# A pre-norm transformer block on one core: normalisation on another engine, masks of the last query block on VectorE, a reordered start and end

## The chip, the cores and the metric

One core of a Trainium2 chip runs the whole program. The time is the device time of one execution in microseconds (us). A core has five engines that run in parallel and meet at semaphores: TensorE (PE, matmuls), VectorE (DVE), ScalarE (ACT), GpSimd (POOL) and SyncE (SP, which here only starts DMAs). TensorE writes to eight PSUM banks of 128 partitions by 512 f32.

## The reference

Eight sequences of 512 tokens with 128 channels go through attention (16 heads of 8 channels, causal) and a feed-forward part with 8 experts that all tokens pass, each weighted by a gate.

```python
def reference(x, w_qkv, b_qkv, w_proj, b_proj, Wg, bg, W1, b1, W2, b2):   # x: 8 x 512 x 128
    x = x + attn(layernorm(x))
    x = x + ffn(layernorm(x))
# attn: q, k, v = split(x @ w_qkv + b_qkv), 16 heads of 8
#       softmax(where(causal, q k^T / sqrt(8), -inf)) v, then @ w_proj + b_proj
# ffn:  probs = sigmoid(x @ Wg + bg);  weights = probs * (probs > 0.5)      # 8 experts
#       h = relu(x @ W1[e] + b1[e])        # 512 hidden
#       sum over e of weights[:, e] * (h @ W2[e] + b2[e])
```

## The kernel before

**Split matmuls.** Where f32 precision is wanted at the speed of the shorter format fp32r, an operand is split in a high part (ACT writes it) and a low part (DVE or POOL subtracts), and three matmuls are added up (L1107 to L1109).

**Attention.** Heads are taken in 4 groups of 4 a sequence. `stack` holds q and k of a group in 32-row pieces, so that the scores of several heads run in different rows of the array at once; even groups lie in rows 0 to 63, odd ones in rows 64 to 127. A group has 10 "max" units and 10 "exp" units, each one PSUM bank. A max unit computes scores with queries on the partitions, adds the causal mask by one more matmul with an identity (L1178, array form 128x128, where the scores' form is 32x128), and DVE takes the negative row maximum (L1018). Units 0 to 3 of a group hold the last query block (`qb == 3`) of one head: 512 keys, of which the last 128 get a mask. Units 4 to 9 hold query blocks 2, 0 and 1. The maxima go through POOL (`nm`, L740, L742), a matmul (L1238), ACT (L819) and two DMAs (L655) into a row of `stack`, so that the exp unit, which computes the scores again with keys on the partitions, has them subtracted. ACT takes the exponential (L831), POOL zeroes the blocks over the diagonal (L755), and 16 small matmuls multiply with v (`pv`, L1248, form 128x32). Then transposes (L1113), a division (L1034, L1038), the projection (L1264).

**A visit** is one call of `scores` on PE: two max units and two exp units that lie some units behind (`EXP_LAG`, 12; 18 for the first 50 units), both or one of them (L1146 to L1179). With 10 units a group, 12 units behind is the group before for 4 of 5 visits, and for the fifth the group before that, which lies in the same rows of the array.

**Layer norm.** DVE computes the statistics (L901, L905), POOL the reciprocal root in two operations (`rs1`, `rs2`: L713, L716), DVE applies both (`ln1n`, `ln2n`: L910, four operations of 128x128), and PE transposes the result (`xT`, `x2T`).

**Feed-forward part.** 32 slots a sequence (8 experts by 4 pieces of the hidden layer). A slot is `z` (three matmuls), ACT's relu into `h_hi` (L863), the low part by DVE (L1070) or, for 12 of 32 slots, by ACT and POOL (L869, L762), and `y` (three matmuls into `y_bank`, L1293 to L1297), which waits for the low part before its first matmul. After four slots DVE multiplies by the gate (`term`, L1083) and POOL adds up (`acc`, L772). `h_hi` and `h_lo` have three buffers.

**What sets the order.** Nothing is scheduled on the chip: `list_schedule` (L279) plays the program through with booked costs and due times when the program is built, and writes down each engine's fixed order. `FFN_LAG` sets how many slots the feed-forward part of a sequence lies behind its attention. Where PE has nothing to do before the first feed-forward work, the list gets `warm` matmuls (L1193), whose result nobody reads. Until then, max units, exp units and W1 preparation share eight banks, afterwards seven and `y_bank`.

**Start.** W1 and the gate weights are multiplied by a centring matrix (`w1`, `small`: L1204 to L1212, ACT L789, DVE L953), to take the mean out of the layer norm. Before the first scores stand the memsets of `stack` on DVE (L878, L879), the load of x, layer norm, transposes, q and k, and the DMAs of `stack` (L641, L644).

Of the kernel before, what the change touches and what calls it, by code (L numbers as in the profile page):

```python
# [44 lines left out]
N_U = len(MAX_UNITS)  # L45
CHUNK_END = (3, 7, 9)
# [5 lines left out]
PT_SLOTS = 14  # L52

# [7 lines left out]
EXP_LAG = 12  # L61
HEAD_LAG, HEAD_UNITS = 18, 50
FFN_LAG = 54
# [4 lines left out]
ENTER = {"full": 190, "mask": 92, "scores": 190, "pv": 98}  # L68
SWITCH_DUE = 1.5
PV_DUE = 2  # L70
# [6 lines left out]
SHIFT = {('act', 'exp', False): 2,  # L77
         ('act', 'hhi', False): 3.5,
         ('act', 'nm', True): -5.5,
         ('dve', 'hlo', False): -7.0,  # L80
         ('dve', 'ln1a', False): 10.0,
         ('dve', 'ln2n', False): 8.5,
         ('dve', 'merge', True): 8,
         ('dve', 'smax', True): -7.5,
         ('dve', 'v', True): 7.5,
         ('dve', 'w1', False): 3.5,
         ('pe', 'ex', True): -9,
         ('pe', 'gate', False): -2.0,
         ('pe', 'gate', True): 0.5,
         ('pe', 'k', False): -4.5,  # L90
         ('pe', 'k', True): -4,
         ('pe', 'nm', False): -35.5,
         ('pe', 'oT', False): -1.5,
         ('pe', 'xT', False): 3,
         ('pe', 'y', False): 1,
         ('pe', 'y', True): 0.5,
         ('pool', 'causal', True): -11.0,
         ('pool', 'nm', True): -14.5,
         ('sp', 'mrow', False): -11}


def visits():

    units = [(i, g, u) for i in range(BATCH) for g in range(GROUPS) for u in range(N_U)]
    result, done = [], 0
    for k in range(0, len(units) + EXP_LAG, 2):
        lag = HEAD_LAG if k <= HEAD_UNITS else EXP_LAG
        while done < k - lag:
            result.append(([], [("ex", *n) for n in units[done:done + 2]]))
            done += 2  # L110
        ex = units[done:done + 2] if done <= k - lag else []
        done += len(ex)
        result.append(([("max", *n) for n in units[k:k + 2]], [("ex", *n) for n in ex]))
    return result


def work_items():
# [20 lines left out]
    put("pool", ("mask", None), -60, 1300)  # L138
    put("pool", ("center", None), -13, 4500, ("pool", ("rs1", 0)))
    put("dve", ("wqk", None), -19.9, 1500, ("dma", ("wqkv", None)), ("dve", ("ln1b", 0)))  # L140
    put("dve", ("b1", None), -13.9, 4200, ("dma", ("small", None)), ("dve", ("klo", 0)))
    put("dve", ("vset", None), -10, 1800, ("dve", ("klo", 0)))
    put("pe", ("small", None), 20, 1500, ("pool", ("center", None)))
    put("dve", ("small", None), 20, 700, ("pe", ("small", None)))
    for e in range(EXPERTS):
        put("pe", ("w1", e), 10 + 2 * e, 1300, ("dma", ("w1", None)), ("pool", ("center", None)),
            ("dve", ("b1", None)), ("pe", ("k", 0)))
        put("act", ("w1", e), 10 + 2 * e, 600, ("pe", ("w1", e)))
        put("dve", ("w1", e), 10 + 2 * e, 690, ("act", ("w1", e)))
# [1174 lines left out]
```

## Time and profile before

| | us |
|---|---|
| median of 3 runs | 685.77 (685.29 to 686.74) |
| the profiled execution | 686.17 |
| its span, from the first to the last instruction | 684.4 |
| PE busy | 650.2 (95%) |
| DVE busy | 480.8 (70%) |
| ACT busy | 418.6 (61%) |
| POOL busy | 330.9 (48%) |

The profiled execution has 1.8 us outside its span, and is 0.4 us above the median. A PE instruction's busy time overlaps the next one's, so what a matmul costs on PE's path is the distance from its start to the start of the next instruction. In a row "x4" stands for four like instructions in a row.

### The profile page before, as it was taken

What the parts mean: (1) busy time and instruction counts of PE and PEld (TensorE: products, weight loads), DVE (VectorE), ACT (ScalarE), POOL (GpSimd) and SP (SyncE); (2) the same over time, 40 slices, a digit from 0 to 9 for tenths busy, and PEclk for the clock granted to TensorE, in tenths of its full rate; (3) what the DMA queues carried; (4) which work ended last, traced back from release to release, by engine and by line L of the source; (5) the groups of instructions that cost most, each with busy time, mean ns of one, the idle gap of its engine ahead of it and who ended that gap; (6) DMA issues with size and microseconds to landing.
All of it is one profiled execution on the core that took longest, in us unless ns stands there. A gap on an engine that the chain in (4) does not pass through costs nothing.

```text
span 684.4 us, 13158 instructions
## 1 busy us (share of the span) xinstructions
PE 650.2 (95%) x4486; PEld 449.4 (66%) x4486; DVE 480.8 (70%) x958; ACT 418.6 (61%) x793; POOL 330.9 (48%) x409
## 2 busy tenths in 40 slices
PE   2799999999999989999999989999999999999996
PEld 2355666667666766667666756667666766677774
DVE  5797687679876796669866696668866676546443
ACT  2158656667666666676666566666666666665553
POOL 4018434556435454556335555455245564545554
PEclk9799999999999999999999999999999999999998
DMA  6442213210322113210222113220222102100310
GB/s 191 111 125 52 51 42 104 57 42 17 87 73 57 41 26 108 69 42 18 86 63 54 40 39 106 57 56 3 59 87 57 42 2 80 48 17 6 103 32 16
DMA packets 29954, 40.44 MB, mean 59 GB/s; under 512 B 4064, under 2 KB 14184, under 8 KB 29888
## 3 DMA queue, kind: packets, MB, share of 16 engines
q1 hardware_dynamic: 29360, 39.40, 21.4%
q8 instruction: 37, 0.61, 0.3%
q10 hardware_dynamic: 528, 0.20, 0.1%
q14 instruction: 29, 0.24, 0.1%
HBM read 23.72 MB, written 2.23 MB: 38 GB/s over the span
## 4 chain that ended last, share of the span: by engine, by line
PE 85%; DVE 6%; issue 3%; DMA 2%; SPq 2%; POOL 1%; ACT 1%; POOLq 0%; DVEq 0%
PE ring L1166 11%; PE ring L1248 10%; PE ring L1107 9%; PE ring L1109 9%; PE ring L1108 9%; PE y_bank L1293 8%; PE y_bank L1297 8%; PE y_bank L1295 8%; PE ring L1178 6%; PE ring L1113 3%; DVE xn L910 2%; PE ring L1193 2%; DVE negmax L1018 1%; DMA g_w<-in_L_ffn_b 1%; PE ring L1228 1%
## 5 line engine op out<-in xcount | busy, mean ns | idle before, releaser
L863 ACT ACTIVATE h_hi<-ring 128x512 fp32r<-128x512 f32 x256 | 153.4, 599 | 126.2 <-PE ring L1109 110.2
L831 ACT ACTIVATE pt<-ring 128x512 f32<-128x512 f32 x313 | 172.0, 596 | 54.7 <-PE ring L1166 51.8
L762 POOL TENSOR_TENSOR h_lo<-h_all,h_hi 128x512 fp32r<-128x512 f32 x96 | 123.9, 1290 | 149.5 <-ACT h_all L869 149.0
L1018 DVE TENSOR_REDUCE negmax<-ring 128x1 f32<-128x512 f32 (+1 forms) x185 | 119.2, 683 | 74.3 <-PE ring L1178 74.2
L1070 DVE SCALAR_TENSOR_TENSOR h_lo<-ring,h_hi 128x512 fp32r<-128x512 f32 x160 | 109.5, 686 | 56.0 <-ACT h_hi L863 52.7
L755 POOL TENSOR_SCALAR_AFFINE_SELECT pt<-pt 128x512 f32<-128x512 f32 x128 | 80.1, 640 | 110.9 <-ACT pt L831 110.8
L1293 PE MATMUL y_bank<-h_hi,w_lo 128*128 128x512 f32 x256 | 109.0, 426 | 1.1 <-DVE f_buf L1083 0.5
L1107 PE MATMUL ring<-x2T_lo,w_hi 128*128 128x512 f32 x256 | 108.0, 422 | 0.3 <-DVE negmax L1018 0.3
L1166 PE MATMUL ring<-stack 32*128 32x256 f32 (+3 forms) x992 | 94.9, 363 | 8.7 <-DMA stack<-stack 4.8
L1297 PE MATMUL y_bank<-h_lo,w_hi 128*128 128x512 f32 x256 | 100.6, 393 | 0.0
L1109 PE MATMUL ring<-x2T_hi,w_hi 128*128 128x512 f32 x256 | 100.5, 393 | 0.0
L1295 PE MATMUL y_bank<-h_hi,w_hi 128*128 128x512 f32 x256 | 99.9, 390 | 0.0
L1108 PE MATMUL ring<-x2T_hi,w_lo 128*128 128x512 f32 x256 | 99.9, 390 | 0.0
L1166 PEld LDWEIGHTS ring<-stack 32*128 32x128 f32 x992 | 55.4, 183 | 61.3 <-issue 55.3
L1018 DVE TENSOR_REDUCE pm<-ring 128x4 f32<-128x512 f32 x123 | 80.7, 681 | 13.0 <-PE ring L1178 12.2
L772 POOL TENSOR_TENSOR f_buf<-f_buf 128x512 f32<-128x512 f32 x56 | 72.2, 1290 | 21.2 <-DVE f_buf L1083 21.2
L1248 PE MATMUL ring<-pt,v_sb 128*32 128x512 f32 (+3 forms) x1024 | 75.5, 436 | 0.0
L1083 DVE SCALAR_TENSOR_TENSOR f_buf<-y_bank,b_cols,f_buf 128x512 f32<-128x512 f32 x64 | 47.9, 748 | 21.5 <-PE y_bank L1297 21.3
L1248 PEld LDWEIGHTS ring<-pt,v_sb 128*32 128x32 f32 x1024 | 30.0, 109 | 47.7 <-issue 42.1
L869 ACT ACTIVATE h_all<-ring 128x512 f32<-128x512 f32 x96 | 56.9, 592 | 0.0
L1293 PEld LDWEIGHTS y_bank<-h_hi,w_lo 128*128 128x128 f32 x256 | 48.2, 188 | 11.9 <-issue 2.0
L1178 PE MATMUL ring<-mask,ident 128*128 128x128 bf16 (+1 forms) x308 | 55.3, 258 | 0.0
(119 smaller groups left out, 754.1 us busy)
## 6 DMA issues: line engine op xcount, KB each, us to landing
f_buf<-gates SPq DMA_DIRECT2D x64, 256.0 KB, 3.3
stack<-parts SPq DMA_DIRECT2D x96, 128.0 KB
x_in<-in_L_attn_x SPq DMA_DIRECT2D x8, 256.0 KB, 2.9
f_buf<-in_L_ffn_W SPq DMA_DIRECT2D x1, 2048.0 KB, 10.4
out_x<-f_buf SPq DMA_DIRECT2D x8, 256.0 KB, 2.3
stack<-nmT SPq DMA_DIRECT2D x64, 8.0 KB
stack<-stack SPq DMA_DIRECT2D x32, 16.0 KB
bv<-in_L_attn_b_qkv SPq DMA_DIRECT2D x1, 256.0 KB
```

What stands on the lines that cost most here:

```text
L762: g_.tensor_tensor(h_lo[:, (i * SLOTS + s) % 3, :], h_all[:], h_hi[:, (i * SLOTS + s) % 3, :].bitcast(F32), ALU.subtract).then_inc(s_hlo_p ...
L831: sc.activation(pt[:, slot, :], b[:], ACT.Exp, scale=SCALE).then_inc(free_sem("ex", i, g, u), 1)
L863: sc.activation(h_hi[:, (i * SLOTS + s) % 3, :], bank_of("z", i, s)[:], ACT.Relu).then_inc(s_hhi, 1)
L1018: v.tensor_reduce(dst, src, AX.X, ALU.max, negate=True).then_inc(free_sem("max", i, g, u), 1)
L1107: mm(dst, hi, x_lo, start=True, stop=False)
L1108: mm(dst, lo, x_hi, start=False, stop=False)
L1109: return mm(dst, hi, x_hi, start=False, stop=True)
L1166: last = mm(out_, lhsT, rhs, start=(k == 0), stop=stop, skip_group_check=True)
L1248: last = mm(b[32 * j:32 * j + 32, kb * P:], v_sb[:, kb, g * GH + j, :], pt[:, slot, col:col + T - kb * P], start=(kb == 0 and g % 2 == 0), ...
L1293: mm(y_bank[:], w2_lo[:, s * C:(s + 1) * C], h_hi[:, (i * SLOTS + s) % 3, :], start=(s % HC == 0), stop=False)
L1295: mm(y_bank[:], w2_hi[:, s * C:(s + 1) * C], h_hi[:, (i * SLOTS + s) % 3, :], start=False, stop=False)
L1297: mm(y_bank[:], w2_hi[:, s * C:(s + 1) * C], h_lo[:, (i * SLOTS + s) % 3, :], start=False, stop=(s % HC == HC - 1)).then_inc(s_y, 1)
```

## The change

- **Layer norm.** `ln1n` and `ln2n` move from DVE to ACT: four activations with the scale and the bias from a column each. POOL computes that bias (two more operations of 128x4 in `rs1` and `rs2`).
- **Masks.** Units with `qb == 3` get no mask matmul; the scores' last matmul releases them. DVE adds the mask in the operation that takes the maximum, which reads a 128x512 bf16 mask beside the bank and writes the bank back.
- **Order of visits.** `EXP_LAG` is 10. Before the first feed-forward work max units and exp units may be visited apart, up to 22 units apart. Booked costs, due times and shifts are other ones. `FFN_LAG` goes from 54 to 59 slots.
- **Feed-forward part.** `y` is two items: two matmuls that wait for `h_hi` alone, and `ylo`, one that waits for the low part, with other work between. `h_hi` and `h_lo` have four buffers. Gate rows are loaded in pairs.
- **Start.** W1 comes in two DMAs and is prepared (5 of 8 experts) before the first scores. The biases of q and k come by one DMA of columns laid out on the host in place of eight; b1 comes over ACT's queue. The memsets of `stack` and `v_sb` are spread over DVE and POOL. The first group's `stack` needs three DMAs, two from SP and one from ACT, not four; the load of x for sequence 2 comes later in SP's queue. v's bias goes into the projection's bias by one matmul. Warm matmuls run before the first transposes.
- **End.** POOL no longer adds the last term: PE adds it by four matmuls into two banks, where the sum so far was put before, and DVE and the output DMA work in halves.

```diff
-EXP_LAG = 12
-HEAD_LAG, HEAD_UNITS = 18, 50
-FFN_LAG = 54
+EXP_LAG = 10
+HEAD_LAG = 22
+FFN_LAG = 59
...
-            put("pe", ("y", i, s), f0 + s + 1.9, 690,
-                ("pool" if s in POOL_SPLITS else "dve", ("hlo", i, s)),
...
+            put("pe", ("y", i, s), f0 + s + 1.9, 460, ("act", ("hhi", i, s)),
                 ("dve", ("term", *divmod((i * SLOTS + s) // HC - 1, EXPERTS))))
+            put("pe", ("ylo", i, s), f0 + s + 2.2, 230, ("pe", ("y", i, s)),
+                ("pool" if s in POOL_SPLITS else "dve", ("hlo", i, s)))
...
+            def normalise(n, i, src, dst, done):
+                act.wait_ge(s_rs[n], i + 1)
+                for t in range(TB):
+                    sc.activation(dst[:, t, :], src[:, t, :], ACT.Identity,
+                                  bias=shift[:, n, t:t + 1],
+                                  scale=rstd[:, n, t:t + 1]).then_inc(done, 1)
...
+                    g_.tensor_scalar(shift[:, n], mv[:, n, :, 0], -1.0, None,
+                                     ALU.mult).then_inc(s_var[n], 1)
...
+                    g_.tensor_tensor(shift[:, n], shift[:, n], rstd[:, n],
+                                     ALU.mult).then_inc(s_rs[n], 1)
...
+                    if qb == 3:
+
+                        v.tensor_tensor_reduce(
+                            out=b[:], in0=causal[:, 0:T], in1=b[:], scale=-1.0, scalar=-MASKED,
+                            op0=ALU.add, op1=ALU.min,
+                            accum_out=negmax[:, g, qb, j % 2, j // 2:j // 2 + 1]
+                        ).then_inc(free_sem("max", i, g, u), 1)
+                        continue
...
+                    for s in range(3 if i or g else 2):
+                        sp.dma_start(rows[s::4, :, :, :], halves(g, s)).then_inc(s_stack[g], 16)
+                    if i:
+                        sp.dma_start(rows[M_ROW::M_STEP, :, 0, :],
+                                     rows[M_ROW + 4::M_STEP, :, 0, :]).then_inc(s_stack[g], 16)
```

PE's list at the program's start, up to the first scores, before: the layer norm's transposes, q, k, v, the gate weights.

```order
L1113 MATMUL ring<-ident,xn 128x128 x4
L1107 MATMUL ring<-xT_lo,wqk_hi 128x512
L1108 MATMUL ring<-xT_hi,wqk_lo 128x512
L1109 MATMUL ring<-xT_hi,wqk_hi 128x512
L1107 MATMUL ring<-xT_lo,wqk_hi 128x512
L1108 MATMUL ring<-xT_hi,wqk_lo 128x512
L1109 MATMUL ring<-xT_hi,wqk_hi 128x512
L1228 MATMUL ring<-wqkv_in,xT 128x128 x4
L1204 MATMUL ring<-ident,g_w 128x8
L1205 MATMUL ring<-wg_in,center 128x8
L1166 MATMUL ring<-stack 128x512 x2
```

The same after, to the second W1 item; L1295 are warm matmuls, L1315 and L1317 prepare one expert of W1.

```order
L1295 MATMUL ring<-causal,ident 128x256 x24
L1212 MATMUL ring<-ident,xn 128x128 x4
L1295 MATMUL ring<-causal,ident 128x256 x2
L1315 MATMUL ring<-g_w,x 128x512
L1317 MATMUL ring<-f_buf,oT 128x512
L1295 MATMUL ring<-causal,ident 128x256 x6
L1206 MATMUL ring<-xT_lo,wqk_hi 128x512
L1207 MATMUL ring<-xT_hi,wqk_lo 128x512
L1208 MATMUL ring<-xT_hi,wqk_hi 128x512
L1206 MATMUL ring<-xT_lo,wqk_hi 128x512
L1207 MATMUL ring<-xT_hi,wqk_lo 128x512
L1208 MATMUL ring<-xT_hi,wqk_hi 128x512
```

Thirty-two warm matmuls and five W1 items now stand before the first scores; v and the gate weights come after them.

A visit on PE in the middle of the program (sequence 2), before. Two max units 0 and 1 (128x512), two exp units of the group two back (128x256, four), the masks, then a slot.

```order
L1109 MATMUL ring<-x2T_hi,w_hi 128x512
L1166 MATMUL ring<-stack 128x512 x2
L1166 MATMUL ring<-stack 128x256 x4
L1178 MATMUL ring<-mask,ident 128x128 x2
L1293 MATMUL y_bank<-h_hi,w_lo 128x512
L1295 MATMUL y_bank<-h_hi,w_hi 128x512
L1297 MATMUL y_bank<-h_lo,w_hi 128x512
```

The same kind of visit after: two max units and exp units 0 and 1 of the group just before, four matmuls.

```order
L1273 MATMUL ring<-stack 128x512 x4
L1398 MATMUL y_bank<-h_hi,w_lo 128x512
L1400 MATMUL y_bank<-h_hi,w_hi 128x512
L1398 MATMUL y_bank<-h_hi,w_lo 128x512
L1400 MATMUL y_bank<-h_hi,w_hi 128x512
L1405 MATMUL y_bank<-h_lo,w_hi 128x512
```

The masks are gone from this visit, the exp units no longer lie in the max units' rows, and the low part's matmul (L1405) stands behind the next slot's first two.

Counted in PE's two lists, in three parts (before first scores; to the first `z`; from there):

| PE's list | before | after |
|---|---|---|
| visits | 0 + 36 + 133 | 0 + 60 + 130 |
| of them with max and exp units in the same rows | 0 + 14 + 25 | 0 + 6 + 0 |
| with two small masks (128x128) / two large (128x256) | 14 / 19, then 50 / 77 | 0 / 21, then 0 / 75 |
| W1 items | 0 + 8 + 0 | 5 + 3 + 0 |
| warm matmuls | 0 + 131 + 0 | 32 + 52 + 0 |

## Rows read from the trace of the kernel before

**Rows 1.** Five stretches: span, busy (count) of five engines, clock, DMA share, GB/s.

```profile
0.00:23.10 23.10, 6.06 (x21) 4.89 (x22) 14.78 (x33) 3.74 (x5) 9.46 (x20) 0.95 0.64 176
23.10:31.60 8.50, 8.48 (x26) 3.75 (x26) 5.53 (x10) 0.60 (x1) 0.00 (x0) 0.52 0.57 131
31.60:100.50 68.90, 66.96 (x603) 41.94 (x602) 54.83 (x134) 43.14 (x86) 29.79 (x47) 1.00 0.27 67
100.50:677.60 577.10, 567.57 (x3836) 398.10 (x3834) 404.19 (x782) 371.11 (x702) 290.41 (x341) 1.00 0.19 53
677.60:684.40 6.80, 1.08 (x4) 0.71 (x4) 1.44 (x2) 0.00 (x0) 1.26 (x1) 0.66 0.12 39
```

**Rows 2.** The start in order of time: start, duration, engine, line, operation, wait before.

```profile
0.79 0.45 SPq L610 DMA_DIRECT2D x_in<-in_L_attn_x  x1
...
5.79 0.80 DVE L901 BATCH_NORM_STATS2 stats<-x_in 128x6 f32<-128x128 f32 x4
...
8.53 1.63 DVE L910 TENSOR_SCALAR xn<-x_in,mv,rstd 128x128 f32<-128x128 f32 x4 [0.34 <-POOL rstd L716]
...
17.06 0.75 DVE L983 SCALAR_TENSOR_TENSOR parts<-ring,bqk,parts 128x512 fp32r<-128x512 f32 x1 [0.53 <-ACT parts L810]
...
18.12 0.38 SPq L630 DMA_DIRECT2D x_in<-in_L_attn_x  x1
...
20.63 0.61 SPq L644 DMA_DIRECT2D stack<-stack  x1
...
23.12 0.79 PE L1166 MATMUL ring<-stack 32*128 32x512 f32 x2 [4.77 <-DMA stack<-stack]
```

**Rows 3.** DMA landing of the first x load (L610).

```profile
DMA to landing us min/median/max: 3.7/3.7/3.7
```

**Rows 4.** PE in order of time: warm matmuls; small masks; same rows; no mask.

```profile
92.59 2.69 PE L1193 MATMUL ring<-mask,ident 128*128 128x256 bf16 x23
...
561.18 0.51 PE L1166 MATMUL ring<-stack 32*128 32x512 f32 x4
561.62 0.28 PE L1178 MATMUL ring<-mask,ident 128*128 128x128 bf16 x2
561.72 0.48 PE L1107 MATMUL ring<-x2T_lo,wg_hi 128*128 128x512 f32 x1
562.03 0.39 PE L1108 MATMUL ring<-x2T_hi,wg_lo 128*128 128x512 f32 x1
562.26 0.40 PE L1109 MATMUL ring<-x2T_hi,wg_hi 128*128 128x512 f32 x1
...
572.44 0.73 PE L1166 MATMUL ring<-stack 32*128 32x512 f32 x6
...
590.69 0.50 PE L1166 MATMUL ring<-stack 32*128 32x256 f32 x4
591.12 0.50 PE L1293 MATMUL y_bank<-h_hi,w_lo 128*128 128x512 f32 x1
591.46 0.39 PE L1295 MATMUL y_bank<-h_hi,w_hi 128*128 128x512 f32 x1
```

**Rows 5.** PE's waits: us in total, times, longest.

```profile
PE ring L1113 <- DVE xn L910: 15.8, 6, 10.3
```

**Rows 6.** Groups by line and shape: count, busy us, mean ns of one.

```profile
L1070 DVE SCALAR_TENSOR_TENSOR h_lo<-ring,h_hi 128x512 fp32r<-128x512 f32 x160 | 109.5, 686 | 56.0 <-ACT h_hi L863 52.7 <-PE y_bank L1297 0.7
...
L1024 DVE TENSOR_REDUCE negmax<-pm 128x4 f32<-128x12 f32 x32 | 5.2, 162 | 2.9
...
L819 ACT ACTIVATE nmT<-ring 32x128 fp32r<-32x128 f32 x32 | 8.4, 263 | 2.2 <-PE ring L1238 2.2
...
L1212 PE MATMUL ring<-f_buf,center 128*128 128x512 f32 x16 | 9.6, 687 | 0.0
```

**Rows 7.** The last stretch in order of time.

```profile
677.62 0.75 DVE L1083 SCALAR_TENSOR_TENSOR f_buf<-y_bank,b_cols,f_buf 128x512 f32<-128x512 f32 x1 [1.05 <-PE y_bank L1297]
...
679.85 1.08 PE L1113 MATMUL ring<-ident,f_buf 128*128 128x128 f32 x4 [2.27 <-POOL f_buf L772]
```

More of the change, by code:

```diff
@@ L71 @@
+PV_DUE = 4
 AFTER_PE, AFTER_OTHERS, AFTER_DMA = 175, 85, 2000
 OVERLAP = {"act": 100, "dve": 85, "pool": 40}
[L77 to L94, printed above, removed]
-         ('pe', 'y', False): 1,
[L96 to L99, printed above, removed]
@@ L102, in visits @@
[L102 to L114, printed above, removed]
+SHIFT = {('act', 'exp', False): 23.0,
+         ('act', 'exp', True): 3.5,
+         ('act', 'nm', False): 15.0,
+         ('act', 'nm', True): -2.5,
+         ('dve', 'klo', False): 4,
+         ('dve', 'merge', False): 8,
+         ('dve', 'merge', True): -2,
+         ('dve', 'qlo', False): 3.0,
+         ('dve', 'smax', False): -4.5,
+         ('dve', 'smax', True): -4,
+         ('dve', 'w1', False): 4.0,
+         ('dve', 'xT', False): 5.0,
+         ('dve', 'yT', True): 7.5,
+         ('pe', 'ex', False): 3.0,
+         ('pe', 'ex', True): -11.5,
+         ('pe', 'gate', False): -11.0,
+         ('pe', 'k', False): 4.5,
+         ('pe', 'max', False): 12.5,
+         ('pe', 'pv', False): 4.0,
+         ('pe', 'q', False): 3.0,
+         ('pe', 'v', False): 4.5,
+         ('pe', 'w1', False): 0.5,
+         ('pe', 'y', False): 1,
+         ('pe', 'y', True): 1.0,
+         ('pe', 'yT', False): 7,
+         ('pe', 'yT', True): 1,
+         ('pe', 'yU', False): 6,
+         ('pe', 'ylo', False): -0.5,
+         ('pool', 'nm', False): 10.5}
@@ L296, in list_schedule @@
     form = "full"
-    masks_made = False
-    score_visits = visits()
+    units = [(i, g, u) for i in range(BATCH) for g in range(GROUPS) for u in range(N_U)]
+    begun = {"max": 0, "ex": 0}
     def at(time, what, key):
@@ L371, in pick_pe @@
                 continue
-            if item[0] != "y" and not free:
+            if item[0] not in ("y", "ylo", "ylast") and not free:
                 continue
@@ L425, in list_schedule @@
                 emptied_at[emptier[key]] = now
-            if key == ("pool", ("mask", None)):
+            if what == "done" and key == ("pool", ("mask", None)):
                 masks_made = True
@@ L1314 @@
     arrays, args = {}, []
-    for name in _INS:
-        a = np.ascontiguousarray(inputs[name])
+    for name, value in laid_out(inputs).items():
+        a = np.ascontiguousarray(value)
         arrays[f"in_{name}"] = a
```

495 lines of the change are left out of this document (292 added, 203 removed).

## The prediction

> **What bounds the kernel now.** I read the stretches first [rows 1], then PE in order of time at three visits [rows 4], then PE's waits [rows 5], and the two ends in order of time [rows 2, 7]. The stretches show five different regimes. Up to 23.1 us PE has done 21 matmuls and waits for everybody: this is a chain of latencies. From 23.1 to 31.6 it is busy throughout at a granted clock of 0.52, that is at the lower of its two levels nearly all the time, after having stood idle for 4.77 us ahead of the first scores [rows 2]. From 31.6 to 100.5 the PE lists attention alone and fills its gaps with 131 warm matmuls. From 100.5 to 677.6, 84% of the span, feed-forward work is there at any time and PE is the bound: 567.6 of 577.1 us busy, while DVE has 404 and ACT 371 us. From 677.6 on nothing overlaps. So a microsecond taken from PE's path is worth one in the fourth stretch, the first and last stretches are worth what their chains lose, and DVE's and ACT's load counts only where it comes near PE's.
>
> I split PE's path of the fourth stretch by distances from start to start. A full matmul of 512 columns takes 0.23 us (562.03 to 562.26), scores of a visit 0.44, two small masks 0.10, and the second full matmul behind masks comes 0.31 us after the first, 0.08 late [rows 4]. With such distances for all items of the fourth stretch the list of before adds up to 564 us; the other 13 are waits. The largest I can name are those of the transposes of `x2T` for DVE's normalisation [rows 5]: 15.8 us in 6 waits, of which the longest, 10.3, is the program's start, so 5 waits share 5.5 us.
>
> **Same rows.** A visit whose max and exp units share rows takes 0.73 where another takes 0.51 [rows 4]: 0.22 more. By the lists there are 14 + 25 such visits before, 6 + 0 after. Fourth stretch: 25 x 0.22 = 5.5 us less; head: 8 x 0.22 = 1.8 less.
>
> **Masks.** 50 visits of the fourth stretch lose their two small masks: 50 x 0.10 = 5.0 less, and 2 fewer large pairs, which I put at 0.15 each, 0.3. But scores without a mask leave the 32-row form directly before a full matmul, whose successor then comes after 0.34 instead of 0.23 us, 0.11 late against 0.08 behind masks [rows 4]. The 50 exits cost 50 x 0.03 = 1.5 more; fewer exits in all give 0.5 back. So this is 4.3 us less, not the 12 that two masks and a whole change of form would suggest. Three fewer visits (0.44 each) and one gate item (three matmuls, 0.7) moved ahead give 2.0; small rest 0.8. Path of the fourth stretch: 564 - 5.5 - 4.3 - 2.0 - 0.8 = 551.4, less 0.9 for the last transposes and the last term, which run in the fifth: 550.5.
>
> **Waits of the fourth stretch.** 13 before. The four operations of L910 took 1.63 us together in the start, beside POOL [rows 2]; ACT's nearest row is 0.263 us for a 32x128 activation [rows 6], so four of them take 1.1 us at least and about 2 at most, if the two column operands double each. The wait for `x2T` can shrink by about as much as it is (5.5) or not at all, where POOL's longer chain eats it. `y` no longer holds PE for the low part, and four buffers let ACT run ahead; that bears on the small waits between slots, some 5 us. I take 7.5 left, with 3 and 14 as ends. Fourth stretch: 550.5 + 7.5 = 558.0, 19.1 less than 577.1.
>
> The operations moved to ACT are weighed against a page. The rows give 1.1 to 2 us for four. The Trainium skill (ScalarE: Activation LUTs, What ACT_TABLE_LOAD costs) says that each per-partition pointer operand adds about 93 ns to an activation and that its cost is 186 ns plus 0.833 ns an element; by that an estimate for one is 0.48 us, and four, overlapping by 93 ns, take 1.64, which is above the 1.13 us that the new list books. Sixteen sets are then 26 us on ACT in place of 18; with the sum as it stands neither changes it, since ACT has room.
>
> **DVE.** It gives up 64 normalising operations and gets 128 mask operations in place of plain maxima. The nearest row is the scalar_tensor_tensor that reads a bank and SBUF, 0.686 us [rows 6]; the order of after shows a second DVE instruction for the accumulated value behind each, nearest the 0.162 us of L1024 [rows 6]. That makes 0.85, between 0.69 (nothing added) and 1.4 (twice, if the write to the bank costs a pass), so 128 x 0.16 = 20 us more against 16 x 1.63 = 26 us less [rows 2]. Balance: nothing, hidden in the fourth stretch under 577 us of PE against 404 of DVE. In the head it is not quite hidden, see below. The Trainium skill (VectorE: DVE Perf Modes, Two Vector instructions with no wait between them) also counts an operation with an accumulator output as two instructions; it speaks against the edit, and no row of before shows its price.
>
> **Start.** x is issued at 0.79 and lands 3.7 us later [rows 2, 3], at 4.5; DVE takes it only at 5.79, behind its memsets. One of these goes to POOL, so statistics start about 4.6: 1.2 us earlier. POOL's two added operations (0.25 each) give back 0.5; ACT normalising instead of DVE, 0. The transposes end at about 10.4. DVE must now do b1 and the split of w_qkv before it can take the low part of x, about 4 us, and b1 comes by ACT's queue: if it lands by 7 this costs nothing, if at 9 then 2 us; I put 0.8. The warm matmuls decide at which clock q and k run: at the upper one six matmuls of 0.23 instead of twice that save 1.4, but one W1 item (9.6 us for 16 matmuls, so 1.2 an item [rows 6]) and eight warm ones stand before q, and cost nothing at the upper clock, up to 1.5 at the lower. From the end of DVE's k part (17.06 + 0.75 = 17.8) to the first scores at 23.12 it is 5.3 us [rows 2]: the load of x for sequence 2 (0.5), three issues, a fourth (0.6), and 1.9 to landing (20.63 + 0.61 to 23.12). After, two issues (1.3) and 1.9: 3.2, which is 2.1 less. Together 1.2 - 0.5 - 0.8 + 1.4 + 2.1 = 3.4: first scores at 19.7, between 17.7 (b1 early, W1 hidden) and 22 (b1 late, lower clock). By then five W1 items are done.
>
> **Head, from first scores to the first z.** Before 77.4 us: 57.3 of work, 131 warm matmuls at 0.115 (2.69 us for 23, the last one's own length taken off [rows 4]) = 15.1, the low clock of 23.1 to 31.6 (half of 8.5) 4.2, and 0.8 of other waits. After: 24 more visits, because max and exp units go apart (24 x 0.44 = 10.6 more), five W1 items less (-5.6 at 1.12), same rows -1.8, masks -1.1, v, the gate weights and one gate item that come later or sooner in the list (2.1 more), changes of form 1.9, rest -0.8: 62.6 of work. 52 warm matmuls, 6.0. The low clock should be gone, since PE works ahead of the first scores. The other waits I put at 4 (1 to 10): DVE has 60.4 us in the two stretches of before [rows 1], and gets nine more maxima at 0.6 and about 30 x 0.16 for masks, less normalising and W1, some 65 of 72.6. First z at 19.7 + 62.6 + 6.0 + 4 = 92.3.
>
> **End.** Before, from DVE's last term (677.62 + 0.75) to the transposes at 679.85 it is 1.5 us, POOL's sum, and four transposes take 1.08 [rows 7]. After, the sum is gone, the first half of PE's and DVE's work is followed by its DMA while the second runs; a second DMA issue comes after the first. 2.0 less: 4.8 for the last 6.8.
>
> **Sum.** 19.7 + 72.6 + 558.0 + 4.8 = 655.1 us of span, with 1.8 outside it 656.9. The profiled execution of before, 686.2, stood 0.4 above the median of its runs; I say **657.0**, 29 less than 685.8: 19 in the fourth stretch, 5 in the head, 3 at the start, 2 at the end.
>
> **Rivals.** (a) *DVE fills up.* If the mask operation takes 1.4 instead of 0.85, it is 128 x 0.55 = 70 us more. In the head some 30 of them add 16 us to 65 of 72.6, which pushes the first z back by about 9; in the fourth stretch DVE's 404 become about 460 of 558, and maxima come late for bank release, 1 us a sequence. 657 + 9 + 8 = 674. For it: the result is written back to the bank, which no row shows. Against: one input is bf16, and reading a bank and SBUF together costs nothing extra in 0.686. (b) *The head and the waits stay.* Units visited apart put 24 more visits into a stretch that was almost full, and the chain maxima to POOL to DMA to exp sets the pace: waits 10 instead of 4, the waits of the fourth stretch stay at 13, the first scores come at 21: 657 + 6 + 5.5 + 1.3 = 670. (c) *Slower: ACT waits for POOL.* ACT's list now stands still at `ln1n` and `ln2n` until POOL's four operations are through, and behind it are relu and exp, on which PE waits one or two slots later. PE has about 1.4 us of cover (two slots of 0.69). To turn a gain of 29 into a loss, each of the 16 normalisations would have to hold PE for 1.9 us or more, so ACT for over 3.3; at 4 us each it gives 657 + 16 x 2.6 = 699. For it: POOL's sums take their turn in the same queue. Against: before, DVE stood at the same place behind the same POOL item, and its waits there are not among the long ones. (d) *Change of form dearer.* If the exit from scores without a mask is not 0.11 but 0.3, as two different forms meet, 76 exits cost 14 more: 671; the rows of 590 to 591 speak against it.
>
> **How the numbers follow.** My forecast's case 0.62; (b) 0.22; (a) 0.10; (d) 0.03; (c) 0.03. The forecast's own range, from the bounds of start (-2.0, +2.3), head (-3, +6) and waits (-4.5, +6.5), taken together in part, is 649 to 665. To reach (b) and most of (a) I set 648 to 672. What a measurement of this kernel tells from no change is about 0.2%, 1.4 us. Faster 0.96, within it 0.01, slower 0.03, which is (c).
>
> **What would show it.** First scores at 18 to 21 us with the clock at its upper level behind; first z near 92; from there to the last y 555 to 562; distances of 0.44 at every visit and none of 0.66; PE's wait for xn from ACT under 3 us outside the start; the mask operation near 0.7 with a second one of about 0.15. The forecast is wrong if z comes after 98, if DVE is over 85% in the fourth stretch, or if ACT waits for `shift` with a queue of relus behind.

## The result, and the profile after

The changed kernel takes **677.61 us** (677.06 to 680.98, four runs) against 685.53 (685.18 to 686.74) for the kernel before: a ratio of 0.9894, 95% interval 0.9878 to 0.9909. That is 8 us less where 29 were forecast, and outside the range of 648 to 672. The profiled execution took 677.06, its span is 675.3.

The stretches of after, as in [rows 1] (span, busy (count) of PE, PEld, DVE, ACT, POOL, then clock, DMA share, GB/s). The bounds are the first scores, three places in the head, the first feed-forward matmul (a gate matmul in both kernels, the forecast's "first z") and a point just behind the start of the last `ylo` (670.06; it ends at 670.45):

```profile
0.00:25.54 25.54, 15.88 (x57) 9.07 (x58) 15.69 (x36) 7.96 (x14) 10.90 (x30) 0.80 0.46 138
25.54:37.40 11.86, 11.25 (x64) 6.65 (x64) 11.35 (x29) 5.09 (x11) 0.44 (x2) 0.98 0.74 186
37.40:57.20 19.80, 16.92 (x72) 8.25 (x74) 10.87 (x29) 9.21 (x18) 7.43 (x10) 0.50 0.23 66
57.20:104.00 46.80, 45.77 (x416) 26.65 (x408) 37.50 (x104) 34.23 (x73) 23.79 (x42) 1.00 0.23 52
104.00:670.10 566.10, 560.27 (x3707) 387.32 (x3708) 373.60 (x821) 386.75 (x744) 296.53 (x362) 1.00 0.19 54
670.10:675.30 5.20, 2.35 (x18) 1.97 (x16) 1.55 (x3) 0.00 (x0) 0.00 (x0) 0.99 0.17 50
```

| stretch | before | forecast | after | missed by |
|---|---|---|---|---|
| to the first scores | 23.1 | 19.7 | 25.5 | 5.8 |
| head | 77.4 | 72.6 | 78.5 | 5.9 |
| fourth stretch | 577.1 | 558.0 | 566.5 | 8.5 |
| end | 6.8 | 4.8 | 4.8 | 0.0 |

In this table the fourth stretch goes to the end of the last `y` or `ylo` in both kernels, as the forecast has it. So there is no one culprit: three places lost 6 to 8.5 us each, and a few rows show where in the first two.

**Start.** DVE, POOL and PE in order of time (start, duration, engine, line, operation, wait before). DVE's f32 to bf16 copy of b1 takes 3.09 us, and POOL's memsets lie over it. W1's first item waits for what follows the copy, and q and k follow that at the lower clock (0.43 us apart in place of 0.23):

```profile
7.59 1.81 POOL L801 MEMSET stack<- 128x2048 f32 x1
8.48 3.09 DVE L1033 CAST g_w<-g_tanh 72x512 bf16<-72x512 f32 x1 [2.92 <-DMA g_tanh<-in_b]
9.48 1.81 POOL L804 MEMSET v_sb<- 128x2048 f32 x1
14.06 0.58 PE L1315 MATMUL ring<-g_w,x 72*128 72x512 bf16 x1 [3.12 <-DVE g_w L1040]
17.85 0.63 PE L1207 MATMUL ring<-xT_hi,wqk_lo 128*128 128x512 f32 x1
18.28 0.63 PE L1208 MATMUL ring<-xT_hi,wqk_hi 128*128 128x512 f32 x1
```

**Head.** SP starts the load of W2 (2 MB, into `f_buf`) ahead of the two small DMAs that carry the row maxima; the issue of these two takes 3.95 us, and PE stands still until they land. From 37.4 to 57.2 the granted clock is 0.50, its lower level, and it was so before that wait began: from 36.9 to 38.9 PE was busy all the time (the last row below is that window). SP's queue in before, where the row maxima go ahead of the load, and then the rows of after:

```profile
36.09 1.13 SPq L655 DMA_DIRECT2D stack<-nmT  x2
41.92 0.83 SPq L648 DMA_DIRECT2D f_buf<-in_L_ffn_W  x1
```

```profile
31.67 0.81 SPq L701 DMA_DIRECT2D f_buf<-in_W  x1
34.39 3.95 SPq L708 DMA_DIRECT2D stack<-nmT  x2
41.78 0.79 PE L1273 MATMUL ring<-stack 32*128 32x512 f32 x2 [2.88 <-DMA stack<-nmT]
36.90:38.90 2.00, 2.00 (x10) 1.04 (x10) 2.00 (x4) 0.00 (x0) 0.00 (x0) 0.50 1.06 293
```

**Fourth stretch.** The two of PE's waits there that matter (us in total, times, longest), to be held against [rows 5]; the first has its longest, 1.9, in the start. The second hardly existed before: 0.5 us in two waits. Then the mask operation and its accumulator read (count, busy, mean ns):

```profile
PE ring L1212 <- ACT xn L870: 3.1, 5, 1.9
PE y_bank L1398 <- DVE f_buf L1174: 2.7, 11, 0.3
```

```profile
L1094 DVE CUSTOM_DVE_ANT_0 ring<-causal,ring 128x512 f32<-128x512 bf16 x124 | 83.3, 713 | 51.8 <-PE ring L1273 51.8
L1094 DVE DVE_READ_ACCUMULATOR2_ANT negmax<- 128x1 f32 x128 | 18.1, 141 | 0.0
```

One more difference shows only when distances are averaged. Two full matmuls in a row, with nothing between, start 0.2298 us apart in before and 0.2330 in after (means over all such pairs closer than 0.26 us in the fourth stretch, 1198 and 1224). Here is the longest undisturbed run of after, its first and last row, 25 distances in 5.82 us:

```profile
618.45 0.39 PE L1400 MATMUL y_bank<-h_hi,w_hi 128*128 128x512 f32 x1
...
624.27 0.39 PE L1208 MATMUL ring<-x2T_hi,w_hi 128*128 128x512 f32 x1
```

### The profile page after: what moved, and what is told of

The parts are those of the page before. It is cut to its first block, busy times and chain, and to the rows that moved or that the text cites. A ratio compares the mean times of both kernels' runs of the same rounds, so it can differ in the third digit from the quotient of the medians.

```text
span 675.3 us, 12981 instructions
## 1 busy us (share of the span) xinstructions
PE 652.4 (97%) x4325; PEld 439.9 (65%) x4325; DVE 450.6 (67%) x1019; ACT 443.2 (66%) x857; POOL 339.1 (50%) x445
## 4 chain that ended last, share of the span: by engine, by line
PE 90%; DVE 3%; ACT 2%; issue 1%; DMA 1%; POOL 1%; SPq 0%; ACTq 0%; DVEq 0%; POOLq 0%
PE ring L1273 11%; PE y_bank L1398 10%; PE ring L1353 10%; PE ring L1206 9%; PE ring L1208 9%; PE ring L1207 9%; PE y_bank L1405 9%; PE y_bank L1400 9%; PE ring L1280 4%; PE ring L1212 3%; DVE f_buf L1174 1%; PE ring L1295 1%; ACT xn L870 1%; PE ring L1369 1%; PE y_bank L1273 1%
## 5 line engine op out<-in xcount | busy, mean ns | idle before, releaser
L1094 DVE CUSTOM_DVE_ANT_0 ring<-causal,ring 128x512 f32<-128x512 bf16 x124 | 83.3, 713 | 51.8 <-PE ring L1273 51.8
L1398 PE MATMUL y_bank<-h_hi,w_lo 128*128 128x512 f32 x256 | 110.8, 433 | 2.7 <-DVE f_buf L1174 2.7
L1206 PE MATMUL ring<-x2T_lo,w_hi 128*128 128x512 f32 x256 | 101.9, 398 | 0.0
L1273 PE MATMUL ring<-stack 32*128 32x384 f32 (+3 forms) x998 | 97.1, 372 | 4.9 <-DMA stack<-nmT 2.9
L1405 PE MATMUL y_bank<-h_lo,w_hi 128*128 128x512 f32 x256 | 100.2, 416 | 0.0
L1273 PEld LDWEIGHTS ring<-stack 32*128 32x128 f32 x998 | 52.0, 186 | 54.2 <-issue 48.1
L1353 PE MATMUL ring<-pt,v_sb 128*32 128x512 f32 (+1 forms) x960 | 70.8, 436 | 0.0
L1353 PEld LDWEIGHTS ring<-pt,v_sb 128*32 128x32 f32 x960 | 28.1, 109 | 45.2 <-issue 39.3
L1206 PEld LDWEIGHTS ring<-x2T_lo,w_hi 128*128 128x128 f32 x256 | 48.2, 188 | 11.8 <-DVE pm L1106 1.0
```

The costliest lines, as they stand in the source:

```text
L1206: mm(dst, hi, x_lo, start=True, stop=False)
L1273: last = mm(out_, lhsT, rhs, start=(k == 0), stop=stop, skip_group_check=True)
L1353: last = mm(b[32 * j:32 * j + 32, kb * P:], v_sb[:, kb, g * GH + j, :], pt[:, slot, col:col + T - kb * P], start=(kb == 0 and g % 2 == 0), ...
L1398: mm(y_bank[:], w2_lo[:, s * C:(s + 1) * C], h_hi[:, (i * SLOTS + s) % H_RING, :], start=(s % HC == 0), stop=False, skip_group_check=True)
L1405: mm(y_bank[:], w2_hi[:, s * C:(s + 1) * C], h_lo[:, (i * SLOTS + s) % H_RING, :], start=False, stop=(s % HC == HC - 1), skip_group_check= ...
```

## The experiments

All kernels at a glance. "Fourth" goes from the start of the first feed-forward matmul to the start of the last `y` or `ylo` matmul, 0.4 us shorter than the stretch in the table above; "spacing" is the mean just told. The time is the median of the timed runs; the other columns are of one profiled execution (it took 667.0 in e1, 669.2 in e5, 662.9 in e10 and 688.2 in e11, apart from the median).

| kernel | time | clock | first scores | first feed-forward | fourth | spacing |
|---|---|---|---|---|---|---|
| before | 685.5 | 0.989 | 23.1 | 100.5 | 576.7 | 0.2298 |
| after | 677.6 | 0.977 | 25.5 | 104.0 | 566.1 | 0.2330 |
| e1 row DMAs first | 675.2 | 0.995 | 24.7 | 94.0 | 566.0 | 0.2330 |
| e2 late memsets | 672.7 | 0.987 | 20.2 | 99.5 | 566.2 | 0.2330 |
| e3 both | 663.5 | 0.997 | 21.0 | 90.4 | 566.3 | 0.2330 |
| e4 PE masks back | 687.4 | 0.985 | 24.5 | 107.2 | 572.4 | 0.2329 |
| e5 = e3 + pad | 665.5 | 0.982 | 22.0 | 98.8 | 563.4 | 0.2302 |
| e6 = before + pad | 688.3 | 0.989 | 23.0 | 100.1 | 579.8 | 0.2328 |
| e7 = after + warm | 672.0 | 0.990 | 25.3 | 98.5 | 566.3 | 0.2330 |
| e8 = e3, y in one | 676.9 | 0.997 | 22.1 | 91.4 | 578.2 | 0.2328 |
| e9 = e5 + warm | 660.0 | 1.000 | 20.1 | 89.4 | 563.1 | 0.2303 |
| e10 = e9 + z ahead of y | 657.2 | 0.987 | 20.3 | 95.6 | 560.3 | 0.2303 |
| e11 = e9, DVE normalises | 682.7 | 0.968 | 25.9 | 107.9 | 573.3 | 0.2304 |

The fourth stretch repeats to 0.3 us from kernel to kernel where its lists are the same. The head doesn't: the granted clock falls in some executions of one program and not in others, and an execution that loses it takes 3 to 8 us more, once 12. Therefore single columns are compared below, and medians only where the spread allows it.

### e1: the row DMAs first

```diff
+_sp = ORDER["sp"]
+_sp.remove(("w2load", None))
+_sp.insert(_sp.index(("mrow", 0, 0)) + 1, ("w2load", None))
```

> The kernel after, with one change in SP's list: the 2 MB load of W2 is issued behind the first two row DMAs (mrow of sequence 0, group 0) instead of ahead of them. Theory A (the load holds up the row DMAs, PE waits, and its clock falls): the second row DMA, whose issue took 3.4 us beside the load, takes 0.5; exp scores start near 38 instead of 41.8 us; the granted clock stays at its upper level, where after shows 0.50 from 37.4 to 56; the first z comes at 94 to 98 instead of 104.8, and the time falls by 6 to 10 us against after's 677.6, to 668 to 672. Theory B (the clock falls because the stretch of single matmuls and waits ahead of the row DMAs exists anyway; the chain maxima to POOL to DMA sets it): the wait shrinks by 2 to 3 us, but 0.50 still shows behind it, and the gain is under 3 us: 675 to 677.

The two issues take 1.19 us in place of 3.95, PE doesn't wait for these two, and the clock holds (SP's queue in order of time, then the windows of the profiled execution):

```profile
33.51 1.19 SPq L711 DMA_DIRECT2D stack<-nmT  x2
35.28 0.82 SPq L704 DMA_DIRECT2D f_buf<-in_W  x1
```

```profile
24.66:37.40 12.74, 12.10 (x72) 7.20 (x72) 12.24 (x30) 5.06 (x11) 0.44 (x2) 1.00 0.41 95
37.40:57.20 19.80, 19.10 (x152) 10.47 (x150) 16.55 (x47) 16.11 (x32) 15.16 (x20) 1.00 0.48 129
```

In the same 19.8 us PE gets through 152 instructions instead of 72, and the feed-forward part begins 10.0 us earlier. This execution took 667.0. But three others took 675.1, 675.2 and 678.9 at mean clocks of 0.98, 0.98 and 0.972. So theory A is right on the DMAs, but early row DMAs don't by themselves keep the clock up. With the clock lost in both kernels, 675.1 against after's 677.6 leaves 2.5 us for the DMAs alone.

### e2 and e3: the memsets late

```diff
                 elif kind == "stackset":
+                    pool.wait_ge(s_wset, 6)
                     g_.memset(stack_half(1), 1.0).then_inc(s_stackset, 1)
```

> The kernel after, with POOL's memsets of the stack and of v held back until VectorE has split w_qkv. Theory A (POOL's memsets hold VectorE's f32 to bf16 copy of b1, 3.09 us instead of 0.59): the copy takes about 0.6, the steps behind it, and with them W1's first item and q, come 2.5 us earlier, first scores at 23.0 instead of 25.5; the rest of the program follows by about as much, 675 us. Theory B (the copy is long by itself, since its input has just landed or its shape of 72 rows costs it): it stays at 3.1 us and the first scores at 25.5; time unchanged, 677.6, or later where the memsets now come in the way of the stack's DMAs.

> Both edits: row DMAs ahead of the load of W2, POOL's memsets behind the split of w_qkv. If both theories hold and their places don't overlap, the gains add up: first scores near 23, first z near 92 to 95, 665 to 669 us. If the clock is lost anyway, only the 2.5 us of the start show, 673 to 675. In the fourth stretch nothing is touched: full matmuls 0.233 us apart, as in after, if that spacing belongs to this kernel's instructions; 0.230, as in before, if it belongs to the chip or the execution.

With POOL silent the same copy takes 0.42 us (e3, DVE, POOL and PE in order of time):

```profile
8.53 0.42 DVE L1037 CAST g_w<-g_tanh 72x512 bf16<-72x512 f32 x1 [2.84 <-DMA g_tanh<-in_b]
12.69 1.81 POOL L805 MEMSET stack<- 128x2048 f32 x1 [4.90 <-DVE wg_lo L999]
13.90 0.47 PE L1210 MATMUL ring<-xT_lo,wqk_hi 128*128 128x512 f32 x1
14.21 0.39 PE L1211 MATMUL ring<-xT_hi,wqk_lo 128*128 128x512 f32 x1
14.44 0.40 PE L1212 MATMUL ring<-xT_hi,wqk_hi 128*128 128x512 f32 x1
```

Theory A holds, and 2.5 us was too little for it: in e2 q starts at 13.05 instead of 17.28 us, now at the upper clock (0.23 apart), and the first scores come 5.4 us earlier. 2.7 of that is the copy; the rest is the clock and the warm matmuls at either level. Together with the row DMAs the head takes 69.4 us in place of 78.5, and e3's four executions lie between 662.8 and 664.4: the gains add up, 14 us by the medians (e2 alone 4.9, e1's one undisturbed execution 10.6). The fourth stretch is as long as in after, and so is the spacing. The latter also answers the question that e3 was to answer: it goes with this kernel's instructions, not with the execution.

The Trainium skill (SBUF — State Buffer, Who interferes with whom) says that VectorE and GpSimd share one pair of ports, and that a VectorE copy or cast in a two-port mode is fully blocked while a GpSimd instruction holds it. The trace agrees: the copy began under the first memset, and ended at 11.57, just after the second large one (9.48 + 1.81 = 11.29).

### e7: the same late DMAs, but PE kept busy

```diff
+_pe = ORDER["pe"]
+_n = _pe.index(("S", [], [(0, 0, 0), (0, 0, 1)]))
+_pe[_n:_n] = [_pe[_n - 1]] * 30
```

> The kernel after with 30 more warm matmuls (about 0.11 to 0.17 us each) in PE's list just ahead of the first exp scores, where PE waits for the row DMAs (37.4 to 41.8 us in after). The row DMAs are as late as in after, only PE is busy meanwhile. It tells the price of the clock from that of the wait. Theory A (the fall of the granted clock to 0.50 behind the idle stretch costs most of the head's loss): the clock stays at its upper level from 42 to 57, first z 5 to 7 us earlier, near 98, time 671 to 673. Theory B (the wait for the row DMAs is the loss, the clock falls anyway or the slow matmuls are hidden beside VectorE's work): first z near 104, time 677.

```profile
37.40:41.80 4.40, 4.40 (x31) 3.51 (x30) 4.13 (x14) 0.00 (x0) 0.00 (x0) 0.74 0.71 200
41.80:57.20 15.40, 15.20 (x121) 8.32 (x121) 9.78 (x24) 12.52 (x25) 11.12 (x15) 1.00 0.07 20
```

Exp scores start at 42.5, even later than in after, and still the feed-forward part begins 5.5 us earlier; all four executions lie within 671.0 to 672.8. The head takes 73.2 us. So of the 9.1 us that e3's is shorter than after's 78.5, 5.3 go with the clock and 3.8 with the wait. The row DMAs didn't bring the clock down, though: in e7 as in after it was at 0.50 by 36.9, before PE's wait for the row DMAs began (38.9), and e5's profiled execution, whose row DMAs are early, stayed at 0.50 over a stretch in which PE was never idle:

```profile
34.00:50.00 16.00, 16.00 (x70) 8.03 (x70) 9.85 (x27) 8.36 (x16) 6.57 (x9) 0.50 0.53 148
```

What e7 shows is the price of the low clock, and that after the 30 warm matmuls at this place it was back.

### e5 and e6: where the streamed operand lies

After has a new tile `shift` of 32 bytes a partition. All tiles allocated behind it, `x2T`, `h_hi` and `h_lo` among them, begin 32 bytes beyond a multiple of 64; in before they begin at a multiple of 64. The weights W1 and W2 lie ahead of it and don't move.

```diff
         shift = sb("shift", [P, 2, TB])
+        pad = sb("pad", [P, 8])
```

> The kernel of e3 with an unused tile of 32 bytes a partition behind `shift`, and nothing else. In after, the new tile `shift` (32 bytes) moves every tile allocated behind it (xT, stack, pt, x2T, h_hi, h_lo and others) from a multiple of 64 bytes to 32 beyond one; the pad moves them back. Full matmuls of the stretch from the first z to the last y stand 0.2331 us apart in after and in e1 to e4, 0.2298 in before. Theory A (the place of the streamed operand decides): the spacing returns to 0.230, the stretch shrinks from 566.1 by 1590 x 0.0033 = 5.2 us to about 561, and the time from 663.5 to 658. Theory B (the spacing comes from something else in the new kernel, such as the waits of the split y, or a ring of four): it stays 0.233 and the time 663.5.

> The kernel before with an unused tile of 32 bytes behind `rstd`, which moves the tiles behind it to 32 bytes beyond a multiple of 64, as in after. Theory A: the spacing of full matmuls goes from 0.2298 to 0.233, the time from 685.4 to 690 or 691. Theory B: no change, 685.4.

The edit does what theory A says, in both directions: 0.2330 to 0.2302 and the fourth stretch 2.9 us shorter in e5; 0.2298 to 0.2328 and 3.1 longer in e6, whose time goes up by a ratio of 1.0049 (1.0033 to 1.0065). The size was put at 5; 3 is what it is. Of the 1590 full matmuls only 1224 have the next one directly behind them, and 1224 x 0.0028 is 3.4. The same run of matmuls as above, in e5, 25 distances in 5.72 us:

```profile
611.26 0.39 PE L1405 MATMUL y_bank<-h_hi,w_hi 128*128 128x512 f32 x1
...
616.98 0.40 PE L1213 MATMUL ring<-x2T_hi,w_hi 128*128 128x512 f32 x1
```

Both kinds of streamed tile take part. Two matmuls in a row on `x2T_hi` are 0.2334 apart in e3 and 0.2300 in e5 (256 pairs each), two on `h_hi` 0.2326 and 0.2294 (150 pairs each).

The median of e5 rose by 2.0 all the same: two executions took 661.3 and 661.8 at a clock of 0.997, two 669.2 and 669.7 at 0.98. The pad hardly moves anything in time; whether the clock falls is close to a toss there.

### e4: PE's share of the masks

```diff
-                        stop = k == len(pieces) - 1 and not (kind == "max" and masked_by_pe(unit))
+                        stop = k == len(pieces) - 1 and not kind == "max"
...
-                for unit in filter(masked_by_pe, mx):
+                for unit in mx:
```

> The kernel after with its lists unchanged, but PE also issues the two small masks of the last query block's units again (VectorE's masking operation stays, so the values are the same). It undoes only PE's share of the mask edit. The prediction's price: about 0.10 us of masks a visit, less 0.03 of exit, 50 to 64 visits in the fourth stretch: 4 to 5 us slower there, and about 1 us in the head, so 682 to 683. Rival: PE's time in those places is cover for waits on ACT or VectorE, so the masks come back for nothing or under 2 us: 678 to 679.

The masks that come back are of 128x256, where before had 128x128, so that, other than the expectation says, the maxima of these units leave out a part of one more key block (they are only a shift under the exponential). By distances a pair of large masks costs 0.148 us and a pair of small ones 0.094 (mean of 47 in before). In the fourth stretch the masks cost 7.5 us more (50 visits), the full matmuls behind them 0.9 less; the stretch as a whole is 6.3 longer. With before's small masks it would be 50 x 0.094 - 0.9 = 3.8, an estimate. That is the prediction's term (4.3 with 0.3 of large pairs in it), confirmed within a microsecond. The rest of the 9.7 us lies in the head (82.7 against 78.5).

### e8: y in one piece

```diff
+_pe = [w for w in ORDER["pe"] if w[0] != "y"]
+ORDER["pe"] = [v for w in _pe for v in ((("y", *w[1:]), w) if w[0] == "ylo" else (w,))]
```

> The kernel of e3, but each slot's two y matmuls on the high part stand directly ahead of the one on the low part again (moved later in PE's list to where the low one is), so that all three wait for the low part as in before; the four buffers stay. The prediction gave the split of y some share of the 5.5 us of waits that go. If it is worth that, the stretch from first z to last y grows by 2 to 5 us, to 568 to 571, and the time to 665.5 to 668.5. If the buffers and the order hide it, 663.5 stays. If splitting costs entries and exits of form, it gets faster, 661 to 663.

It costs 11.9 us against e3, far more than the 2 to 5 expected, and half of that are waits of the transposes for ACT's copies (1.1 in after):

```profile
PE ring L1218 <- ACT o_grp L950: 7.1, 14, 1.8
```

These lists were planned for a split `y`, so 12 is an upper bound for its worth.

### e9 and e10: the last fault found

After's z to y step in order of time (PE). The start of an expert's `y` waits for DVE's term of the expert before. It comes 0.40 us late by distances (0.63 in place of 0.23), and its second matmul 0.08 more; that happens eleven times, all of them behind 588 us:

```profile
642.49 0.39 PE L1208 MATMUL ring<-x2T_hi,w_hi 128*128 128x512 f32 x1
643.12 0.47 PE L1398 MATMUL y_bank<-h_hi,w_lo 128*128 128x512 f32 x1 [0.24 <-DVE f_buf L1174]
643.43 0.40 PE L1400 MATMUL y_bank<-h_hi,w_hi 128*128 128x512 f32 x1
```

At these places nothing but one `z` (0.70 us) stands between the end of an expert and the start of the next. Before has two such places, and PE waits for the term at both; elsewhere two `z` or other work stand there. e9 adds 20 warm matmuls to the start of e5; e10 adds to e9:

```diff
+for _p in range(len(_pe) - 8):
+    _a, _b, _c = _pe[_p:_p + 3]
+    if _a[0] == "ylo" and _a[2] % 4 == 3 and _b[0] == "z" and _c[0] == "y" and _c[2] % 4 == 0:
+        _q = _p + 3
+        while _pe[_q][0] in ("y", "ylo"):
+            _q += 1
+        if _pe[_q][0] == "z":
+            _pe.insert(_p + 2, _pe.pop(_q))
```

> The kernel of e5 (row DMAs first, late memsets, pad) with 20 more warm matmuls where PE stood idle in the start: 4 ahead of the transposes of x, 8 ahead of the first W1 item, 8 ahead of the first scores. In e5 two executions of four took 661.3 and 661.8 at a mean granted clock of 0.997, two took 669.2 and 669.7 at 0.98; the profiled one shows 0.50 from 36 to 50 us. Theory A (the clock falls by chance of what PE did in the start's gaps, so filled gaps keep it up): all executions lie near 661, with q and k at the upper clock first scores near 20.5 and 0.5 to 1 us less, 660 to 661. Theory B (the fall comes from the sparse stretch around 30 to 33 us, where VectorE is the bound and nothing is added): the spread stays, 661 to 670.

> The kernel of e9; at nine places of the last part, where PE's list has one z between the end of one expert's y and the start of the next one's, the next z is moved ahead of that start. In after PE waits there eleven times for VectorE's term (0.24 us shown, 0.40 with the late second matmul). Theory A (the split let the start of y come one z earlier than the term is ready; this is the new wait in the old one's place): nine waits go, 9 x 0.4 = 3.6 us less between first z and last y, 563.2 to 559.6, and 3.6 less than e9. Theory B (the wait only moves to the next item, since VectorE or the ring of banks sets the pace there): under 1 us.

e9: three executions took 659.5 to 660.1 at full clock, one 665.7 at 0.986. So filled gaps in the start don't rule the loss out; e10's profile, below, has it from 31.8 us on. e10: the fourth stretch is 2.8 us shorter, of 3.6 expected, and its waits for the term fell from eleven to two (PE's waits of e10):

```profile
PE y_bank L1416 <- DVE f_buf L1192: 0.5, 2, 0.2
```

The profiled execution of e10 is the one of five that lost the clock (662.9). The other four took 657.03 to 657.45. Its windows show where:

```profile
32.00:50.00 18.00, 18.00 (x90) 8.71 (x90) 11.57 (x30) 10.30 (x20) 8.52 (x11) 0.53 0.48 133
50.00:95.60 45.60, 44.60 (x399) 26.10 (x392) 36.97 (x103) 33.13 (x71) 22.87 (x41) 1.00 0.24 54
95.60:655.90 560.30, 554.88 (x3707) 388.09 (x3708) 373.45 (x821) 386.89 (x744) 296.26 (x362) 1.00 0.19 54
```

e10 beats both kernels: 0.9591 of before (0.9572 to 0.9609).

### e11: VectorE normalises again

```diff
+for _now, _engine, _item in [s for s in STARTS if s[1] == "act" and s[2][0] in ("ln1n", "ln2n")]:
+    _next = next(s[2] for s in STARTS if s[0] >= _now and s[1] == "dve")
+    ORDER["act"].remove(_item)
+    ORDER["dve"].insert(ORDER["dve"].index(_next), _item)
...
+                    v.tensor_scalar(dst[:, t, :], src[:, t, :], mv[:, n, t, 0:1],
+                                    rstd[:, n, t:t + 1], ALU.subtract, ALU.mult).then_inc(done, 1)
```

> The kernel of e9 with every normalisation moved back from ScalarE to VectorE, each at the place in VectorE's list that was planned for the same moment; the other lists unchanged. It undoes that part of the change alone. The prediction: before, PE's waits for xn were 5.5 us in five places of the fourth stretch, and ScalarE's taking over was to save up to that. If so, 3 to 6 us slower between first z and last y. Rival: with the new lists VectorE has the room, and the waits of before came from its list, not from the engine: within 1 us of e9. A dearer case: in the head, where VectorE is full from 22 to 36 us, it adds another 1 to 2.

The fourth stretch is 10.2 us longer. Not all of it is the normalisation: the granted clock is at its lower level from the stretch's start to 113.8, and matmul by matmul against e9 that costs 1.3 us.

```profile
107.80:113.80 6.00, 5.91 (x21) 3.30 (x25) 4.12 (x15) 3.40 (x7) 4.65 (x8) 0.50 0.33 74
```

The other 8.9 come in six steps of about 1.5, one a sequence; before lost 5.5 in this way. The start is 5.8 longer, and that comes from the place in DVE's list: the four operations stand behind b1's steps and begin at 11.73, ACT's in e9 at 7.77. Before itself shows why an operation of 0.33 us (its minimum there) holds PE for 1.28: four of them take 2.48 us, and POOL's subtraction of 1.29 lies over them.

```profile
321.21 2.48 DVE L910 TENSOR_SCALAR xn<-x,mv,rstd 128x128 f32<-128x128 f32 x4
321.22 1.29 POOL L762 TENSOR_TENSOR h_lo<-h_all,h_hi 128x512 fp32r<-128x512 f32 x1
...
323.83 0.63 PE L1113 MATMUL ring<-ident,xn 128*128 128x128 f32 x4 [1.28 <-DVE xn L910]
```

And e11 (DVE, POOL, PE): its first four with POOL silent in the start, then four beside POOL's subtraction, and behind them in DVE's list the low part of x, for which the next transposes wait, 7.0 us in five waits:

```profile
11.73 1.12 DVE L1009 TENSOR_SCALAR xn<-x_in,mv,rstd 128x128 f32<-128x128 f32 x4
...
238.12 2.47 DVE L1009 TENSOR_SCALAR xn<-x,mv,rstd 128x128 f32<-128x128 f32 x4
238.99 1.27 POOL L861 TENSOR_TENSOR h_lo<-h_all,h_hi 128x512 fp32r<-128x512 f32 x1
240.52 0.68 DVE L1076 TENSOR_TENSOR xT_lo<-ring,xT_hi 128x512 fp32r<-128x512 f32 x1
241.25 0.66 PE L1227 MATMUL ring<-ident,xn 128*128 128x128 f32 x4 [1.40 <-DVE xT_lo L1076]
```

The longest of these operations lasts 1.47 us in before and 1.32 in e11. ACT's never wait for POOL in this way (mean 0.48 to 0.50 in after). The four take 2.47 us beside POOL and 1.12 with POOL silent, and the 1.35 between them is nearly the whole of PE's wait of 1.40. So by these rows most of the gain of moving the normalisation is that it gets out of POOL's way, and little of it is DVE's time; no run moves POOL's subtraction instead.

## Why the prediction was wrong

The working got the arithmetic of PE's path nearly right, and missed what the new lists do to each other at four places. With these mended, e9's start and head and e10's fourth stretch and end give 20.1 + 69.3 + 560.7 + 4.9 = 655.0 of span, where the forecast said 655.1, and undisturbed executions of e10 take 657.0 to 657.5. That the sums agree so closely is luck: the head is 3.3 better than forecast, the fourth stretch 2.7 worse, the start 0.4 and the end 0.1.

- **Same rows.** Right. Before has 25 visits of 0.666 us (start to start) in the fourth stretch, where others take 0.44; after has one. All scores of the stretch take 7.1 us less; the forecast had 5.5, and 1.3 for three visits fewer.
- **Masks.** Right: 3.8 by e4 against 4.3. The exit without a mask costs 0.34, as read from [rows 4]; rival (d) is out.
- **Waits of the fourth stretch (13 to 7.5).** This step failed. The waits for `xn` went as said: 5.5 us before, some 1.2 after. The transposes of x still start up to 0.4 late behind masks. Some 5 us of new waits came, for DVE's term (eleven of 0.48 by distances; e10 wins back 2.8). I credited the split of `y` with shorter waits and didn't ask what its earlier start would wait for next. What the normalisation is worth was under-sized: e11 puts it at 8.9 with these lists.
- **Spacing of full matmuls.** The sum took 0.23 for granted. 0.003 more at every full matmul with another behind it is 3 us (e5, e6), and it comes from one tile of 32 bytes that the diff shows. No step of mine looked at addresses.
- **Start.** The statistics began 1.5 us earlier (4.28 against 5.79), the transposes ended at 10.5 (forecast 10.4). The term for b1 (0.8, "if at 9 then 2") failed: b1 landed at 8.5, and the copy then took 2.7 us longer because of the memsets, which the change had moved to POOL and I had counted as free. Behind it the clock of q and k was the lower one; the sum had 1.4 saved there. From stack's issue to the scores it is 3.9 (21.66 to 25.54), not 3.2.
- **Head.** "The low clock should be gone" failed. That SP's list has the load of W2 ahead of the row DMAs now, and behind them before, stood in the order of the two kernels; I counted neither as a move past a queue. The wait cost 2.5 to 3.8 (e1, e3 against e7). The low clock, from 36.9 on, cost 5.3 (e7), and why it fell stays open: it fell before that wait, and in e5 and e10 without it. With the row DMAs first and the clock up, 69.3 is under the forecast of 72.6, so 4 for other waits was too much.
- **DVE.** Right: 0.713 + 0.141 against 0.85, and 451 us busy of 675. Rival (a) is out. ACT waited 7.9 us for POOL's `shift` in all, 3.2 of it in the start, and hardly passed it on; rival (c) is out.
- **End.** Right: 4.8 against 4.8; the second half's transposes start 1.0 behind the first's (670.29, 671.29).
- **Rival (b)** named the place of the loss (head and waits stay), not its cause; its 670 was nearer but still too low, and its chance of 0.22 was too small. What was missing in all cases is the time that a reordered list loses at places no row of before shows. Three such places of 3 to 6 us each would have been a fair allowance.

**Open.** What decides in a given execution whether the clock falls behind 30 us isn't settled. From 26 to 30 us PE is busy 3.47 us of 4.00 and DVE all the time in e9's profiled execution, which kept the clock, and the same in e10's, which lost it at 31.8. Whether SP's queue or the DMA engines, whose share is 1.06 from 36.9 to 38.9, held up the row DMAs behind the load of W2 wasn't told apart. Why a start 32 bytes beyond a multiple of 64 widens the spacing no run shows, nor whether other offsets do. The 2.7 us by which e10's fourth stretch is above the forecast aren't split further.

## What to carry over

When a change reorders lists, go along every queue for small transfers that now stand behind a large one, and along POOL's list for memsets that lie beside VectorE's copies; both cost several us here and were visible before any run. When a tile is added or removed, see where the tiles behind it now begin. And when a wait is removed by starting an item earlier, look up which of its other inputs comes last then.

## What the runs showed of the hardware

- A VectorE copy of 72x512 f32 to bf16: 0.42 us with POOL silent, 3.09 beside two large POOL memsets. A VectorE normalisation of 128x128: 0.33 alone, up to 1.47 beside a POOL subtraction.
- The issue of two small DMAs: 1.19 us alone, 3.95 behind a 2 MB load on the same queue.
- Streamed tiles that begin 32 bytes beyond a multiple of 64: full matmuls of 512 columns 0.2328 to 0.2330 us apart instead of 0.2298 to 0.2304, in both kernels and both directions.
- The same program kept TensorE's upper clock in some executions and lost it in others. By their mean granted clocks, e5 kept it in 2 of 4, e1 in 1 of 4, e3 in 4 of 4; an execution that lost it took 3 to 8 us more, once 12. Where it is down, PE can be busy throughout at 0.50 for 16 us (e5, 34 to 50).
